# Layer 0 for four pairs of samples at once, two pairs to a PSUM bank, and a reordered start, in a two-layer conditional residual kernel

## The reference, cut to what matters

```python
# x: (128, 64, 512); w: (8, 64, 64); W: (512, 512); A: (8, 16, 512); Bm: (8, 512, 16)
h = x + einsum('bct,bcd->bdt', x, w[subject]) + bias[subject][:, :, None]     # layer 0
H = einsum('btd,od->bto', h, W)                                                # layer 1
delta = einsum('btr,bor->bto', einsum('btd,brd->btr', h, A[adapter]), Bm[adapter])
out = h + H + delta * scalings[adapter][:, None, None]
```

## Time and profile before

| what | us |
|---|---|
| median of three runs (264.48 to 266.23) | 265.62 |
| the profiled execution | 265.84 |
| its span, first to last instruction | 264.2 |
| PE busy | 241.5 |

### The profile page before, as it was taken

The page is one execution under the profiler, slowest core; times in us unless marked ns, Lnnn a source line. Parts: engine busy times, 40 slices in busy tenths (PEclk is TensorE's granted clock), DMA queues, the critical chain, the costliest instruction groups (busy, mean ns, idle before and its releaser), DMA issues.

```text
span 264.2 us, 9940 instructions
## 1 busy us (share of the span) xinstructions
PE 241.5 (91%) x2929; PEld 194.7 (74%) x2930; DVE 145.2 (55%) x244; ACT 113.4 (43%) x189; POOL 82.2 (31%) x284
## 2 busy tenths in 40 slices
PE   0463999899999999999999999999999999999993
PEld 0442888688788888888888887888878887887882
DVE  5657557755565666755575655566675554433200
ACT  2154345544454445444464444544544443333411
POOL 6332342533324333332343332432333333320000
PEclk9977699999999999999999999999999999999999
DMA  6663144555545554655455545555564445552231
GB/s 114 152 186 105 43 133 134 160 139 148 154 144 156 157 159 139 180 154 144 121 177 155 141 140 146 157 152 159 139 188 149 144 127 179 155 156 79 70 78 42
DMA packets 25826, 36.69 MB, mean 139 GB/s; under 512 B 6736, under 2 KB 8784, under 8 KB 25808
## 3 DMA queue, kind: packets, MB, share of 16 engines
q1 hardware_dynamic: 20400, 28.06, 37.2%
q10 hardware_dynamic: 5408, 8.40, 12.3%
HBM read 19.67 MB, written 16.78 MB: 138 GB/s over the span
## 4 chain that ended last, share of the span: by engine, by line
PE 86%; DVE 5%; DMA 3%; issue 2%; ACT 1%; SPq 1%; ACTq 0%; DVEq 0%
PE ps L717 69%; PE ps L702 13%; PE ps L682 2%; DMA x_ring<-in_x_dram 2%; PE ps L664 2%; DVE m_lo L487 1%; DMA ids_i<-in_itok_B_dram 1%; DVE m_f L481 1%; ACT m_hi L563 1%; DVE x L494 0%; ACT x_hi L569 0%; DVE place L453 0%; DVE prec_n L388 0%; PE ps L654 0%; DVE x_lo L502 0%
## 5 line engine op out<-in xcount | busy, mean ns | idle before, releaser
L717 PE MATMUL ps<-m_hi,x_hi 128*128 x264 | 106.9, 405 | 0.8 <-DVE m_lo L487 0.8
L717 PE MATMUL ps<-m_lo,x_hi 128*128 x264 | 103.5, 392 | 0.0
L717 PE MATMUL ps<-m_hi,x_lo 128*128 x264 | 103.4, 392 | 0.0
L502 DVE TENSOR_TENSOR x_lo<-x,x_hi 128x512 fp32r<-128x512 f32 x64 | 44.5, 695 | 86.5 <-ACT x_hi L569 86.5
L359 POOL COPY p_pair<-p_all 64x64 f32 x128 | 45.6, 356 | 135.0 <-DVE x L494 62.0
L578 ACT ACTIVATE o_ring<-ps 128x512 f32<-128x512 f32 x60 | 35.8, 597 | 63.2 <-PE ps L717 62.9
L717 PEld LDWEIGHTS ps<-m_hi,x_hi 128*128 128x128 f32 x264 | 49.9, 189 | 12.6 <-issue 1.6
L717 PEld LDWEIGHTS ps<-m_hi,x_lo 128*128 128x128 f32 x264 | 49.8, 189 | 10.8
L569 ACT ACTIVATE x_hi<-x 128x512 fp32r<-128x512 f32 x64 | 40.4, 632 | 39.8 <-ACT o_ring L578 18.6
L717 PEld LDWEIGHTS ps<-m_lo,x_hi 128*128 128x128 f32 x264 | 49.9, 189 | 9.5
L702 PEld LDWEIGHTS ps<-p_pair,x_ring 64*64 64x64 f32 x2048 | 34.2, 139 | 18.2 <-issue 16.5
(11 more groups left out here) (81 smaller groups left out, 55.5 us busy)
## 6 DMA issues: line engine op xcount, KB each, us to landing
x_ring<-in_x_dram SPq DMA_DIRECT2D x128, 128.0 KB, 2.6
out_dram<-o_ring ACTq DMA_DIRECT2D x64, 128.0 KB, 2.4
out_dram<-o_ring SPq DMA_DIRECT2D x64, 128.0 KB, 2.5
o_ring<-in_L_cond_W_dram SPq DMA_DIRECT2D x4, 256.0 KB, 4.6
a_f<-in_L_cond_A_dram SPq DMA_DIRECT2D x8, 128.0 KB
b_nat<-in_L_cond_Bm_dram SPq DMA_DIRECT2D x1, 256.0 KB, 4.1
p_all<-in_L_cond_weights_dram SPq DMA_DIRECT2D x2, 128.0 KB, 4.3
bias_all<-in_fside_8xS_dram SPq DMA_DIRECT2D x1, 256.0 KB, 5.7
```

What stands on the lines that cost most here:

```text
L502: nc.vector.tensor_tensor(x1_lo[:, u % HELD], x1[:, u % 2], x1_hi[:, u % HELD], ALU.subtract).then_inc(x1_lo_ready, 1)
L717: mm = nc.tensor.matmul(ps[:, bank, :], part[:, u % HELD, c, :], m[:, ds(k * (TC * T) + c * T, T)], start=(c == 0 and part is x1_hi and m ...
```

## The change

- `AHEAD` goes from 6 to 7: in step j SP asks for the x of pair j+7. A slot is waited for by the count of finished layer 0s in their new order.
- Layer 0 is done in groups of four pairs 4q to 4q+3 (called a quad below), in the order 4q, 4q+2, 4q+1, 4q+3, at PE's step 4q-2. Before, two pairs were done in each even step. The first four pairs are still done two and two.
- Two pairs share a bank: pair 4q takes columns 0 to 255 of banks 0 and 1, pair 4q+2 columns 256 to 511 of the same banks, the odd pairs likewise in banks 6 and 7. `x1_add` of an even pair waits for both even layer 0s of its quad, that of an odd pair for all four.
- `layer0_inputs` is called for all four pairs before `words`: PE waits for four x, four POOL copies, and the `x1_add`s of the whole quad before.
- At the start PE turns the last part of W and makes the third and fourth tile product before the layer 0 of pairs 0 and 1; DVE and ACT take their tile work in the matching order.
- The step contents of POOL and the numbers of buffers are unchanged.

```diff
--- before.py
+++ after.py
@@ -45,7 +45,8 @@
     MIXED = K // 2
     XR = 4
     OR = 4
-    AHEAD = 6
+    AHEAD = 7
+    L0_QUAD = 4
     HELD = 4
     W_BATCH, W_AHEAD, W_SUBJECT, W_PLACE = 0, 2, 4, 6
 
@@ -122,9 +123,16 @@
         ps = ctx.enter_context(nc.psum_tensor("ps", [P, 8, 512], F32))
         b_turned_at = ps[:, 4, :].rearrange("p (c n) -> p n c", c=TC)
 
-        def l0_banks(u):
-
-            return 6 * (u % 2)
+        def l0_count(j, u):
+
+            if isinstance(j, int) and j < L0_QUAD:
+                return j + 1
+            return j - u % L0_QUAD + (2, 4)[u % 2]
+
+        def l0_out(u):
+
+            cols = TC * C * (u // 2 % 2)
+            return ps[:, 6 * (u % 2):6 * (u % 2) + 2, cols:cols + TC * C]
 
 
         ids_in = sem("ids_in")
@@ -248,7 +256,8 @@
 
             def load_x(j, slot, b):
 
-                at_least(sp, l0_done, j - XR + 1)
+                at_least(sp, l0_done, j - XR + 1 if isinstance(j, int) and j < XR + L0_QUAD
+                         else j - XR - slot + (1, 3, 2, 4)[slot])
                 for half in range(2):
                     sp.dma_start(x_ring[C * half:C * half + C, slot, :], x[ds(b[half], 1)]
                                  .rearrange("b c t -> (b c) t")).then_inc(x_in[slot], 16)
@@ -488,11 +497,10 @@
 
             def x1_add(j, u):
 
-                dve.wait_ge(l0_done, j + 1)
+                dve.wait_ge(l0_done, l0_count(j, u))
                 at_least(dve, x1_lo_ready, j - 1)
-                bank = l0_banks(u)
                 nc.vector.tensor_tensor(x1[:, u % 2].rearrange("p c (h d) -> p c h d", h=2),
-                                        ps[:, bank:bank + 2, 0:TC * C].rearrange("p h (c d) -> p c h d", c=TC),
+                                        l0_out(u).rearrange("p h (c d) -> p c h d", c=TC),
                                         bias_pair[:, u % XR, :].rearrange("p (h d) -> p h d", h=2).unsqueeze(1)
                                         .to_broadcast([P, TC, 2, C]), ALU.add).then_inc(x1_ready, 1)
 
@@ -509,14 +517,14 @@
             m_add(0, 0)
             m_add(1, 1)
             m_split(0, 0)
+            m_split(1, 1)
+            m_add(2, 2)
+            m_add(3, 3)
             x1_add(0, 0)
-            m_add(2, 2)
+            m_split(2, 2)
             x1_split(0, 0)
-            m_split(1, 1)
-            m_add(3, 3)
-            m_split(2, 2)
+            x1_add(1, 1)
             m_split(3, 3)
-            x1_add(1, 1)
             x1_split(1, 1)
 
             def step(j, u, n):
@@ -616,8 +624,8 @@
             copy_wt(3)
 
             act.wait_ge(warmed, 1)
+            m_round(2, 2)
             x1_round(0, 0)
-            m_round(2, 2)
             m_round(3, 3)
             x1_round(1, 1)
             act.wait_ge(batches_ready, 1)
@@ -688,21 +696,29 @@
                 pe.wait_ge(x_in[slot], after(j, u, 32))
                 pe.wait_ge(pair_ready, j * 4 + 4)
 
-                at_least(pe, x1_ready, j - 1)
+                at_least(pe, x1_ready, j - 1 if isinstance(j, int) and j < L0_QUAD else j - u % L0_QUAD)
 
             def layer0(j, u):
 
                 slot = u % XR
-                bank = l0_banks(u)
+                x1_t = l0_out(u)
                 for c in range(TC):
                     for side in range(2):
                         for half in range(2):
                             rows = slice(C * half, C * half + C)
                             at = c * P + side * C
-                            mm = nc.tensor.matmul(ps[side * C:side * C + C, bank + half, c * C:c * C + C],
+                            mm = nc.tensor.matmul(x1_t[side * C:side * C + C, half, c * C:c * C + C],
                                                   x_ring[rows, slot, at:at + C], p_pair[rows, slot, :],
                                                   start=True, stop=True)
                 mm.then_inc(l0_done, 1)
+
+            def l0_at(j, u):
+
+                if isinstance(j, int) and j == 0:
+                    return range(2, L0_QUAD)
+                if u % L0_QUAD == 2 and (not isinstance(j, int) or j + 2 < PAIRS):
+                    return (2, 4, 3, 5)
+                return ()
 
             def layer1(j, u, k, bank, done=l1_done, tiles_awaited=False):
 
@@ -727,25 +743,24 @@
             m_product(0, 0)
             m_product(1, 1)
             turn_w(2)
-            layer0_inputs(0, 0)
-            layer0(0, 0)
             turn_w(3)
             m_product(2, 2)
             m_product(3, 3)
             pe.wait_ge(others_ready, 2)
+            layer0_inputs(0, 0)
+            layer0(0, 0)
             layer0_inputs(1, 1)
             layer0(1, 1)
             regs = [pe.alloc_register(f"pe_word{i}") for i in range(2)]
 
             def step(j, u, n):
                 mixed = n_of_mixed(j) is not None
-                if u % 2 == 0 and (not isinstance(j, int) or j + 2 < PAIRS):
-                    layer0_inputs(j + 2, u + 2)
-                    layer0_inputs(j + 3, u + 3)
+                l0_pairs = l0_at(j, u)
+                for i in l0_pairs:
+                    layer0_inputs(j + i, u + i)
                 k = words(pe, regs[:2 if mixed else 1], table[0:1, ds(j * 8 + W_PLACE, 2 if mixed else 1)], K - 1)
-                if u % 2 == 0 and (not isinstance(j, int) or j + 2 < PAIRS):
-                    layer0(j + 2, u + 2)
-                    layer0(j + 3, u + 3)
+                for i in l0_pairs:
+                    layer0(j + i, u + i)
                 if makes_parts(j, u, n) is not None:
                     turn_b(makes_parts(j, u, n))
                 if n is not None and u == HEAD + 1:
```

## The result

The changed kernel takes 292.68 us (median of 4 runs, 292.05 to 295.81) against 265.35 us before; the ratio is 1.105 (95% interval 1.097 to 1.114). The forecast was 293. The profiled execution took 292.05 us, its span is 290.4.

What follows compares the result with a forecast made beforehand. PE, busy 91%, was taken as the bound, with new waits for POOL's copies: 6 x 1.1 + 18.6 + 1.5 - 1.3 + 0 = 25.4 us on 265.84, 291.2; one clock fall of 2.1 gives 293 us, range 282 to 302.

Steps and rivals of the forecast that it cites:

- The chain that sets a group's start: From E through ACT, DVE and POOL's last copy, then the table read, to layer 0: E + 7.3 or E + 9.8.
- E: End of layer 1 of pair 4q-1, taken at the start of the tile product behind it.
- A quads: Quads starting at u = 0, six in the loop: PE waits 1.3 us for POOL, each costs +1.1 us.
- B quads: Quads starting at u = 4, where x1_add stands behind splits awaiting A's rows: +3.1 us each, six make 18.6.
- The wait at u = 5: In B quads PE waits 0.8 us before layer 1 of u = 5 for a tile, inside the +3.1.
- The start: New order begins layer 0 of pairs 2 and 3 2.5 us sooner; POOL's 1.4 and the larger group's 1.1 cancel it.
- The clock: PE's clock falls to its lower level in one of the six B quads: +2.1 us.
- the two quads of the tail: They build no tiles; between 0 and 1.1 us each, 1.5 us taken for both.
- The gain of the switches: Fifteen fewer switches into and out of layer 0 at 0.2 us each: 3.0 us, counted inside the quad terms.
- cold-after-every-wait rival: The clock falls after every B quad's wait, 6 x 2.1 = 12.6 us on 291.2: 303.8 us; chance 0.14.
- rival in which loads decide: The landing of x, not POOL's copies, sets when groups start: 276 us; chance 0.06.
- the read stays hidden: PE's table read behind the waits of a group costs nothing: 10 us less, 281 us; chance 0.05.

Runs made afterwards that it cites:

- pool8: The changed kernel with eight slots instead of four for POOL's copies: 278.45 us.
- words_first: The changed kernel with PE's table read moved ahead of the waits of a group: 285.4 us.
- per_pair: The changed kernel with the table read first and each pair's waits right ahead of its own layer 0: 269.25 us.
- early_split: per_pair with DVE's m_split moved ahead of x1_split in each step: 264.5 us, ratio 0.9955 to the kernel before.
- pairs_pool: early_split with eight slots for POOL's copies, groups of two pairs, one pair to a bank, x six ahead: 261.15 us; with groups of four 260.56 us.
- ahead6: The changed kernel with x asked for six pairs ahead instead of seven: 339.0 us.
- quads_only: The changed kernel with the start order of the kernel before; groups of four and x seven ahead stay: 297.86 us.

## Why the prediction was right, step by step

Two rows of the start of the changed kernel, the layer 0 of pairs 2 and 3 and turn_b behind it, against the earlier trace rows:

```profile
23.66 1.16 PE L710 MATMUL ps<-p_pair,x_ring 64*64 64x64 f32 x64 [3.62 <-DVE x L502]
24.75 1.07 PE L672 MATMUL ps<-ident,b_dup 128*128 128x128 f32 x4
```

- *The chain that sets a group's start.* Right in place and nearly in size: E + 7.6 measured for 7.3 (A), E + 10.2 for 9.8 in the B quad shown. pool8, words_first and per_pair each took one link away, and gave 14.2, 7.3 and 23.4 us where 15, 8 to 10 and 25 were expected of them. That each acts is shown; the closeness of the first and the last is partly luck, as their parts show.
- *A quads, +1.1.* From group to group the four without a fall of the clock take 15.07 to 15.18 us (forecast 15.1).
- *B quads, +3.1.* Too high for most. Five of the six take 17.79, 16.67, 16.88, 16.83 and 17.97 us from group to group (forecast 17.6); 17.23 is the mean, 0.4 below. The term was off by taking the landing of A's rows at 71.89, where ACT begins to round them at E + 4.2, for all. In the changed kernel it begins at E + 3.5 to 3.7 in three of these bodies, and PE waits 1.2 to 1.35 us for POOL; in the other two it begins at E + 4.6 and 4.8, and PE waits 2.2 and 2.4. The sixth, the first of the loop, takes 18.24 us where before it took 15.86, with two waits of 1.0 us, for an m_add and for a copy_out, that the account did not have.
- *The wait at u = 5.* Forecast 0.8, measured 1.1, inside the B sum as said. per_pair and early_split showed that it becomes a cost of its own once POOL is out of the way.
- *The start.* The first group of four was worked out 1.1 us sooner than the 35.39 of before, and starts at 34.46, 0.9 sooner, but both halves of that were larger: turn_b begins at 24.75 and ends at 25.82, both 2.9 us sooner than before (forecast 2.5). 2.0 of that are the order (23.66 for 25.69). 0.8 are the clock, which here fell only behind 24, when the layer 0 of pairs 2 and 3 was all but done: it took 1.16 us and not 1.99. POOL took back 2.0 and not 1.4: the group starts 8.6 us behind the end of turn_b, where 8.1 was forecast and 6.7 was before.
- *The clock.* One fall at 2.1 us was taken; there were two, at about 1.5 us each (a quad with one takes 16.6 instead of 15.1). The price had been read at the start of before, up to 30.00. The windows show 0.61 from 30 to 31, so that fall lasted to about 30.8 and cost some 2.5 us. There it came ahead of the work; in the loop it came just after the group had begun.
- *The sum.* 27.5 us were forecast on the profiled execution and 26.2 came. In group starts: A quads 6.8 (forecast 6.6), B quads 15.8 (18.6), clock 3.0 (2.1), the two quads of the tail 2.1 (1.5), the start -0.9 (-1.1), what is behind the last group -0.5 (-0.2, from the -1.3 and the 1.09 of that group's two more pairs). So the B term was 2.8 too high, and the clock and the tail made up about half of it. The medians are 27.3 us apart, 1.1 more than the profiled executions; that brought the measured 292.7 as close to 293 as it is, and is luck.
- *The gain of the switches.* The 3.0 us for fifteen switches were never seen as such. In an unwaited A quad 0.36 was measured for one switch against pairs_pool, and 0.27 against before (13.71 and 13.98 us), somewhat over the 0.2 read from the earlier trace rows. The B quads give it back, and the total of grouping is nil within the measurement (pairs_pool).
- *The rivals.* The cold-after-every-wait rival did not hold for this kernel: 2 of 14 groups fell to the lower clock, both behind B waits, so 2 of 6 B quads. In ahead6, with waits of 2.2 to 4.1 us, eleven of fifteen did. The Trainium skill was cited for this rival (TensorE: Matmul & The Clock Gate, "HAM oscillation"). The kernel described there waits some 3 to 5 us between bursts and starts each of them cold; most waits of ahead6 are that long, those of the changed kernel, 2.4 us at most, are not. The prediction also took before to have one long idle stretch; PE had waited 4.5 and 5.3 us as well, up to 10.05. The windows give 1.00 behind those, yet the turn_b at 10.46 takes 1.11 us, as long as at the lower clock at 27.61, so the clock shown there is doubtful. The rival in which loads decide had 276 us, and pool8 measured 278, but with loads named as releaser in only part of the groups. That the read stays hidden was refuted by words_first.

## What to carry to other kernels

Before work is put into larger groups, work out for the last member of a group when its inputs come free, going through every engine that recycles a buffer for it; a rotation of four buffers gives a group of four no room at all, though the group of two had two steps of it. If a group has to be, read tables ahead of its waits and wait for each member right before it: that alone took back 23 of 27 us here, 4 of them at the start. And price the grouping by itself: the switch it saves was 0.2 to 0.4 us.

## What the runs showed of the hardware that I had not expected

The granted clock after a wait of PE goes with the length of the wait, but not strictly. Taking the groups of four of the changed kernel, of quads_only, words_first and ahead6 together: none that had waited up to 1.85 us ran at the lower level; all seven with waits of 1.97 to 2.66 us did; of the thirteen with waits of 3.1 us and more, all in ahead6, ten did and three kept the full clock. I have no account for these three. The group of two in step 0 waited 2.7 to 4.5 us, and the clock fell around it in each of these kernels, but in the changed kernel and ahead6 only some 1 us after its matmuls had begun. Each fall cost the work behind it some 1.5 us, so a wait near 2 us is worth more than its own length, and the spread of the runs of one kernel (292.05 to 295.81) goes with it in part: the granted clock of those two runs was 0.982 and 0.968.
